# Attention plus causal convolution on one core: the out projection from exact f32 matmuls to three f32r products

## The reference, cut to what matters

```python
# x (16, 512, 1024); mask = cond (16, 1024)
q = xt @ Wq.T                                    # per batch 1024 x 512, 8 heads of 64
scores = scale * q_h @ q_h.T                     # keys = queries = values
logits = (scores * cmask + (1.0 - cmask) * -1e30) * rmask
ctx = softmax(logits) @ q_h
x = x + (ctx @ Wo.T) transposed                  # the out projection and the residual
x = x + causal_depthwise_conv(x, cond) + bias
```

## Time and profile before

| | us |
|---|---|
| median of 3 runs | 4175.13 (4171.65 to 4175.92) |
| profiled execution, its own time | 4174.45 |
| its span, first to last instruction | 4172.7 |
| TensorE busy in the span | 4055.7 (97%) |
| ScalarE busy | 2709.2 (65%) |
| GpSimd busy | 2543.2 (61%) |
| VectorE busy | 2417.5 (58%) |
| share of 16 DMA engines, main queue | 42.5% |

### The profile page before, as it was taken

How to read it: one execution, slowest core, us unless ns; L and a number is a source line. 1 busy time by engine, 2 the same in 40 slices (tenths; PEclk the granted TensorE clock), 3 DMA queues, 4 the chain that set the end, 5 groups by cost and what they waited for, 6 DMA issues and landing times. The chain is left out here.

```text
span 4172.7 us, 57357 instructions
## 1 busy us (share of the span) xinstructions
PE 4055.7 (97%) x18688; PEld 2506.5 (60%) x18688; DVE 2417.5 (58%) x2260; ACT 2709.2 (65%) x3782; POOL 2543.2 (61%) x1042
## 2 busy tenths in 40 slices
PE   7999999999999999999999999999999999999799
PEld 4665656566565655655565665556556555655598
DVE  4664555556565655656565565656556465656676
ACT  4775757667575766757576675757667575766465
POOL 4775767667575766757576675757667575766200
PEclk8999999999999999999999999999999999999999
DMA  4433434343343434344343434434433443443588
GB/s 111 106 87 91 104 94 114 91 105 92 91 105 88 117 92 101 92 94 104 86 117 92 101 92 93 108 83 117 97 97 92 97 106 81 116 97 76 147 292 265
DMA packets 308543, 451.95 MB, mean 108 GB/s; under 512 B 155043, under 2 KB 223267, under 8 KB 308134
## 3 DMA queue, kind: packets, MB, share of 16 engines
q1 hardware_dynamic: 308262, 448.18, 42.5%
HBM read 112.28 MB, written 67.11 MB: 43 GB/s over the span
## 5 line engine op out<-in xcount | busy, mean ns | idle before, releaser
L725 POOL TENSOR_TENSOR plo<-p,phi 128x1024 fp32r<-128x1024 f32 x1024 | 2539.3, 2491 | 1349.0 <-ACT phi L656 1344.1
L654 ACT ACTIVATE p<-sc 128x512 f32<-128x512 f32 x2048 | 1108.9, 594 | 815.9 <-PE sc L527 676.1
L769 DVE TENSOR_REDUCE mrow<-misc 128x1 f32<-128x1024 f32 x1024 | 1203.0, 1216 | 731.2 <-PE misc L488 731.1
L656 ACT ACTIVATE phi<-p 128x1024 fp32r<-128x1024 f32 x1024 | 1086.1, 1061 | 32.5
L526 PE MATMUL sc<-quer,keys 128*128 128x512 f32 x2048 | 912.1, 445 | 22.9 <-issue 13.1
L539 PE MATMUL pv<-phi,val 128*96 128x512 f32 x2048 | 857.5, 419 | 18.3 <-issue 18.3
L527 PE MATMUL sc<-quer,keys 96*128 96x512 f32 x2048 | 810.8, 396 | 0.0
L541 PE MATMUL pv<-phi,val 128*64 128x512 f32 x2048 | 806.4, 394 | 0.0
L545 PE MATMUL pv<-plo,val 128*96 128x512 f32 x2048 | 639.0, 393 | 0.9 <-POOL plo L725 0.9
L539 PEld LDWEIGHTS pv<-phi,val 128*96 128x96 f32 x2048 | 330.1, 161 | 339.7 <-issue 184.6
L526 PEld LDWEIGHTS sc<-quer,keys 128*128 128x128 f32 x2048 | 387.7, 189 | 192.5 <-issue 69.0
(11 more groups left out here) (70 smaller groups left out, 2823.7 us busy)
## 6 DMA issues: line engine op xcount, KB each, us to landing
keys<-hi SPq DMA_DIRECT2D x256, 256.0 KB, 3.2
quer<-mhi SPq DMA_DIRECT2D x256, 256.0 KB, 5.0
keys<-lo SPq DMA_DIRECT2D x128, 256.0 KB, 5.7
quer<-mlo SPq DMA_DIRECT2D x128, 256.0 KB, 3.8
xo<-x SPq DMA_DIRECT2D x64, 512.0 KB, 4.8
x<-xo SPq DMA_DIRECT2D x64, 512.0 KB, 4.9
xin<-x SPq DMA_DIRECT2D x16, 2048.0 KB, 13.4
out<-stage SPq DMA_DIRECT2D x64, 512.0 KB, 6.4
```

The costliest lines, as they stand in the source:

```text
L654: act.activation(p32[:, t % NP32, half(h)], sc[:, h, :], ACT.Exp, scale=SCALE).then_inc(s_p32, 1)
L656: act.activation(phi[:, t % NPHI, :], p32[:, t % NP32, :], ACT.Copy).then_inc(s_phi, 1)
L725: pool.tensor_tensor(plo[:, t % NPLO, :], p32[:, t % NP32, :], phi[:, t % NPHI, :].bitcast(F32), ALU.subtract).then_inc(s_plo, 1)
L769: reduced = dve.tensor_reduce(mrow[:, q:q + 1], misc[:, k, :], AX.X, ALU.max)
```

## The change

- `wo` (f32) goes. At the start the weight is loaded into the memory of `xo`, ScalarE writes its high part `woh` (one copy of 128 x 2048 to F32R), VectorE its low part `wol`.
- `ct` goes. The normalisation writes in place into `ca`. After the exponentials of step (p, 1, 7), ScalarE copies `ca` of the pair before to `cth[:, p]` (F32R, 128 x 1024), and after its `plo` of that step GpSimd makes `ctl[:, p]` = `ca` - `cth`.
- An out item is 12 f32r matmuls instead of 4 f32 ones: woh x cth, wol x cth, woh x ctl, 4 blocks each.
- The out items stand at other steps, and the stores of `xo` at other places of SyncE's queue.
- In the tail, high and low parts of the last pair are made by ScalarE and VectorE by halves, after both halves have been normalised.
- Memory is laid out anew (`val`, `mneg`, `mask8r` placed over the convolution's tiles, `spare` added, a smaller scratch for dynamic DMA).

```diff
-OUT_AT = {(0, 1, 7): 0, (1, 0, 0): 1, (1, 0, 2): 2, (1, 0, 4): 3,
-          (1, 0, 6): 4, (1, 1, 0): 5, (1, 1, 2): 6, (1, 1, 4): 7}
+HIGH_AT = (1, 7)
+LOW_AT = (1, 7)
+OUT_AT = {(1, 0, 2): 0, (1, 0, 3): 1, (1, 0, 5): 2, (1, 0, 7): 3,
+          (1, 1, 0): 4, (1, 1, 2): 5, (1, 1, 3): 6, (1, 1, 5): 7}
...
-                sp.dma_start(wo[:], woT.rearrange("(k p) e -> p k e", p=P)).then_inc(s_const, 16)
+                sp.dma_start(wo32, woT.rearrange("(k p) e -> p k e", p=P)).then_inc(s_woh, 16)
...
-                        if phase != "first" and (p, i) == (1, 0):
-                            store_xo(b - 1, 0)
                         if phase != "first" and (p, i) == (1, 1):
+                            store_xo(b - 1, 1)
                             load_xo(b - 1, 3, True)
...
                         if phase != "first" and (p, i) == (1, 0):
+                            store_xo(b - 1, 0)
                             load_xo(b - 1, 2, True)
-                            store_xo(b - 1, 1)
...
-                if phase == "end" and item[1] == 0:
-                    pe.wait_ge(s_half, 1)
-                elif item[1] == (1 if phase == "end" else 0):
-                    pe.wait_ge(s_cnorm, PAIRS * (prev_b + 1))
-                for k in range(PAIRS):
-                    last = pe.matmul(out, wo[:, k, m * P:(m + 1) * P], ct[:, k, half(h)],
-                                     start=(k == 0), stop=(k == PAIRS - 1))
+                if phase == "end":
+                    if item[1] < 2:
+                        pe.wait_ge(s_last_ctl, item[1] + 1)
+                elif item[1] == 0:
+                    pe.wait_ge(s_ctl, PAIRS * (prev_b + 1))
+                cols = slice(m * P, (m + 1) * P)
+                for n, (w, c) in enumerate(((woh, cth), (wol, cth), (woh, ctl))):
+                    for k in range(PAIRS):
+                        last = pe.matmul(out, w[:, k, cols], c[:, k, half(h)],
+                                         start=(n == 0 and k == 0), stop=(n == 2 and k == PAIRS - 1))
...
-                    act.wait_ge(s_cnorm, pair(b, p) - 1)
+                    act.wait_ge(s_ctl, pair(b, p) - 1)
...
+            def context_high(b, p):
+                act.wait_ge(s_cnorm, pair(b, p) + 1)
+                if not (isinstance(b, int) and b == 0):
+                    act.wait_ge(s_xo, b * 2 * DT)
+                act.activation(cth[:, p, :], ca[:, p % 2, :], ACT.Copy).then_inc(s_cth, 1)
...
+                act.wait_ge(s_woh, 16)
+                act.activation(woh[:], wo32, ACT.Copy).then_inc(s_wo_high, 1)
...
                             exponentials(b, p, i, t, first)
+                            if (i, t) == HIGH_AT and not (phase == "first" and p == 0):
+                                context_high(*before(b, p))
...
+            def context_low(b, p):
+                pool.wait_ge(s_cth, pair(b, p) + 1)
+                pool.tensor_tensor(ctl[:, p, :], ca[:, p % 2, :], cth[:, p, :].bitcast(F32), ALU.subtract).then_inc(s_ctl, 1)
...
                             split(b, p, i, t, phase == "first" and p == 0 and i == 0)
+                            if (i, t) == LOW_AT and not (phase == "first" and p == 0):
+                                context_low(*before(b, p))
...
-                dve.tensor_tensor(ct[:, p, :], ca[:, p % 2, :], den[:, p % 2, :], ALU.mult).then_inc(s_cnorm, 1)
+                dve.tensor_tensor(ca[:, p % 2, :], ca[:, p % 2, :], den[:, p % 2, :], ALU.mult).then_inc(s_cnorm, 1)
...
+            def weights_low():
+                dve.wait_ge(s_wo_high, 1)
+                dve.tensor_tensor(wol[:], wo32, woh[:].bitcast(F32), ALU.subtract).then_inc(s_wol, 1)
...
-                    dve.tensor_tensor(ct[:, p, half(h)], ca[:, p % 2, half(h)], den[:, p % 2, half(h)], ALU.mult).then_inc(done, 1)
+                    c = ca[:, p % 2, half(h)]
+                    dve.tensor_tensor(c, c, den[:, p % 2, half(h)], ALU.mult).then_inc(s_last_norm, 1)
+                for h in range(2):
+                    dve.wait_ge(s_last_cth, h + 1)
+                    if h == 0:
+                        dve.wait_ge(s_ctl, PAIRS * B - 1)
+                    dve.tensor_tensor(ctl[:, p, half(h)], ca[:, p % 2, half(h)], cth[:, p, half(h)].bitcast(F32),
+                                      ALU.subtract).then_inc(s_last_ctl, 1)
```

More of the change, by code:

```diff
@@ L131, in __init__ @@
             self.quer = sb("quer", [P, 4, T], F32R, place)
+            self.mneg = sb("mneg", [KT, P], F32R, place)
+            self.mask8r = sb("mask8r", [KT, P], F32R, place)
         self.xin = sb("xin0", [P, SLOTS, TH], F32)
@@ L140, in __init__ @@
             self.p32 = sb("p32", [P, NP32, T], F32, place)
+            self.val = sb("val", [P, 2, KT, 2, VC], F32R, place)
         with ExitStack() as place:
@@ L146, in __init__ @@
         self.brow = sb("brow", [P, T], BF16)
+        self.spare = sb("spare", [P, 2560], F32)
         self.own = sb("own", [P, CH], F32)
@@ L199, in build_attention @@
         wq = sb("wq", [P, DT, D], F32)
-        wo = sb("wo", [P, PAIRS, D], F32)
+        woh = sb("woh", [P, PAIRS, D], F32R)
+        wol = sb("wol", [P, PAIRS, D], F32R)
         ident_r = sb("ident_r", [P, P], F32R)
@@ L214, in build_attention @@
         keys, quer, keys2, quer2 = pre.keys, pre.quer, pre.keys2, pre.quer2
-        val = sb("val", [P, 2, KT, 2, VC], F32R)
+        val = pre.val
         mrow = sb("mrow", [P, KT], F32)
-        mneg = sb("mneg", [KT, P], F32R)
-        mask8r = sb("mask8r", [KT, P], F32R)
+        mneg, mask8r = pre.mneg, pre.mask8r
         p32, phi, plo = pre.p32, pre.phi, pre.plo
@@ L222, in build_attention @@
         den = sb("den", [P, 2, T], F32)
-        ct = sb("ct", [P, PAIRS, T], F32)
+        cth = sb("cth", [P, PAIRS, T], F32R)
+        ctl = sb("ctl", [P, PAIRS, T], F32R)
         xo = sb("xo", [P, 2, T], F32)
+        wo32 = xo[:].rearrange("p a t -> p (a t)").rearrange("p (k e) -> p k e", e=D)
         sc = ps("sc", [P, 2, HALF])
@@ L231, in build_attention @@
         s_begin = sem("s_begin")
-        s_half = sem("s_half")
         s_ident = sem("s_ident")
@@ L259, in build_attention @@
         s_cnorm = sem("s_cnorm")
+        s_woh = sem("s_woh")
+        s_wo_high = sem("s_wo_high")
+        s_wol = sem("s_wol")
+        s_cth = sem("s_cth")
+        s_ctl = sem("s_ctl")
+        s_last_norm = sem("s_last_norm")
+        s_last_cth = sem("s_last_cth")
+        s_last_ctl = sem("s_last_ctl")
         s_ones = sem("s_ones")
@@ L566, in start @@
                 do("start", 0, 0, "head", PHASES["start"]["head"], (0, 0, 0))
-                pe.wait_ge(s_const, 32)
+                pe.wait_ge(s_const, 16)
             def batch(phase, b):
@@ L573, in batch @@
                             first = phase == "first" and p == 0 and i == 0
+                            if phase == "first" and (p, i, t) == (1, 0, 0):
+                                pe.wait_ge(s_wol, 1)
                             scores(b, p, i, t, first)
@@ L681, in end @@
                     last_context(h)
+                p = PAIRS - 1
+                for h in range(2):
+                    act.wait_ge(s_last_norm, h + 1)
+                    act.activation(cth[:, p, half(h)], ca[:, p % 2, half(h)], ACT.Copy).then_inc(s_last_cth, 1)
             run(act, start, batch, end)
@@ L838, in start @@
                 do("start", 0, 0, "head", PHASES["start"]["head"], (0, 0, 0))
+                weights_low()
             def batch(phase, b):
@@ L891, in end @@
                 p = PAIRS - 1
-                for h, done in enumerate((s_half, s_cnorm)):
+                for h in range(2):
                     dve.wait_ge(s_cab, NH * B + h)
@@ L1082 @@
     from concourse.bass_utils import run_bass_kernel_spmd
-    nc = bacc.Bacc("TRN2", target_bir_lowering=False, num_devices=1)
+    nc = bacc.Bacc("TRN2", target_bir_lowering=False, num_devices=1, dynamic_dma_scratch_size=1024)
     arrays = {
```

## The result

Median 4107.99 us (4105.77 to 4113.86, 4 runs) against 4174.38 (4 runs) before: ratio 0.9844, interval 0.9827 to 0.9861. Forecast was 4111. The profiled execution took 4113.86, its span is 4112.1, 60.6 less than before.

| stretch | before | after | change | forecast |
|---|---|---|---|---|
| start to the first exponential | 43.51 | 43.77 | +0.26 | 0 |
| steps, to ScalarE's first copy of the last context | 3850.04 | 3785.17 | -64.9 | -65.5 |
| tail, to the convolution's first memset | 45.19 | 49.55 | +4.4 | +1.8 |
| convolution | 233.96 | 233.61 | -0.35 | 0 |

What follows compares the result with a forecast made beforehand. TensorE was taken to bound the steps, the chain of VectorE and transfers the tail. From 4174.45 us: -75.6 items, +9.6 waits, +0.5 parts, +1.8 tail gave 4110.8, said as 4111; own range 4102 to 4122, widened to 4094 to 4130.

Steps and rivals of the forecast that it cites:

- Items: Out items on TensorE: 2.80 us each instead of 3.43, 75.6 us saved over the 120 in steps.
- Rival D: Out items: f32r products of this shape run at an f32 record's distance, about 4385 us; chance 0.01.
- Waits around moved items: TensorE's waits in pair 1 and after: 2.0 us against 1.36, 0.64 given back a batch, 9.6 in 15.
- W: Time for pairs 1 and 2 together, mneg of step (0, 1, 5) to that of (2, 1, 5); 134.31 us before.
- rival A: Steps: waits do not grow, or the next step absorbs them; 4081 to 4102 us, chance 0.13.
- Parts in step (p, 1, 7): High and low parts on ScalarE and GpSimd: covered, cost 0; 0.5 us charged for the last batch's pair 3.
- Start: Making the weight's parts before the first exponential and maxima: cost 0, at worst 2 us.
- Tail: Between attention and convolution: low parts on VectorE delay its chain; cost 1.8 us, between 0 and 4.7.
- Total: Whole kernel: -63.7 us against the profiled 4174.45, so 4110.8; said as 4111.

Runs made afterwards that it cites:

- f32 items: Changed kernel with each out item as four f32 matmuls of the high parts alone, high and low parts still made; 4177.9 us, ratio 1.0006.
- places alone: Kernel before with only the out items' steps and the order of SyncE's queue changed, items left as four f32 matmuls; 4175.5 us, ratio 1.0001.
- mhi and lo first: Changed kernel with VectorE making mhi and lo before the residual in step (1, 0, 2); 4092.1 us, ratio 0.98.
- either remedy: Changed kernel with mhi and lo before the residual in (1, 0, 2), 4092.1 us, or with out items 0 to 2 at (1, 0, 4) to (1, 0, 6), 4098.3 us.
- all three: Changed kernel with mhi, lo before the residual, tail low parts on GpSimd, items 0-3 in even steps from (1, 0, 0), 30 useless tail matmuls; 4097.4 us.
- two products: Changed kernel without the product wol x cth, so 8 f32r matmuls an item instead of 12; 4067.6 us, ratio 0.9739.
- mhi and lo first, tail on GpSimd: Changed kernel with mhi and lo before the residual in (1, 0, 2) and the tail's two low parts made by GpSimd; 4086.4 us, ratio 0.9792.

## Why the prediction was right

- **Items.** 12 x 0.233 = 2.80 was met to the last digit, and f32 items and places alone confirm that nothing else carries the gain. Rival D (5.15) is out, and so are the 2.57 that the prediction worked out from the four passes in the Trainium skill, *FP8 and Floating Point Precision*, section TensorE Precision Notes.
- **Waits around moved items.** 1.52 for item 1: step (1, 0, 3) takes 7.48, and 5.94 once the wait is removed (mhi and lo first), so 1.5; it is gone with either remedy. Step (1, 0, 1) is 0.36 longer than before, for 0.37, and (1, 1, 0) takes 6.02 against 5.93 in all three, for 0.1. W was forecast as 76.7 + 53.2 = 129.9 and is 129.83. One bound of this part is added up wrongly: no waits at all would be 2.0 x 15 = 30 us better than the forecast and not 20, which is the distance from unchanged waits (rival A has it right).
- **Parts in step (p, 1, 7).** 0 forecast; W differs by 0.03 between f32 items and places alone. For the last pair, which has no projection, 0.5 was charged; from the `mneg` of (2, 1, 5) to that of (3, 0, 5) it is 23.29 against 23.12.
- **Start.** 0 forecast; +0.26, which says nothing: over all runs the first exponential starts between 42.3 and 44.5, at 42.80 in places alone.
- **Tail.** The mis-sized term: 1.8 forecast, 4.4 measured. The step that failed is "at 2.80 each the first residual is due as the tap table ends". The item took 5.26 at the lower clock, behind 10.74 us of an idle TensorE, and VectorE waited 2.73 for it. The lower clock was there before as well: the item began behind 6.12 of idle, and from 3899.6 to 3903.0 the granted clock was 0.50. But then the residual started at 3905.62, right behind the tap table, with no idle time shown, so VectorE's work hid the slow item. The stretch had shown the clock at 0.84 there, and I did not use it. The size varies: in the changed kernel run again the clock came back during the item, which took 4.18, and the tail 48.36.
- **Total.** 4110.8 forecast from the profiled execution of before; the one of after took 4113.86, 3.1 more, of which 2.6 are the tail. The median lies 6 below it, by scatter between executions: on the stretch over a change of batch (from the `mneg` of (3, 1, 5) to that of the next (0, 1, 5)) the mean over 14 batches was 55.30 in the profile after and 54.91 in the same kernel run again.
- **Luck.** That the steps came out at -64.9 for -65.5 is in part luck. W summed over 15 batches fell by 67.6, more than the forecast's 66.0; some 3.5 of this was given back, since the clock fell at four changes of batch in the profile after and at two in that of before (last section).

## What to carry to other kernels

Where an instruction of VectorE with two SBUF inputs may meet one of GpSimd, work out both starts relative to what anchors each: making the work ahead of one shorter can move it into the other's time, and then lose most of what was saved. A chain that a bank's turn leads through (reduction, bank, matmul) turns such a hold into idle time of TensorE, and a turned order on VectorE was enough to avoid it here. Work that is hidden behind another engine's wait should be looked up for every place where it runs: the one pair without a projection gave up 7.6 us where its fellows gave 0.14. Add the items' price from distances between starts, and give an item that begins behind a long idle time of TensorE (4.3 and 10.7 us here) the price at its lower clock.

## What the runs showed that I had not expected

- Saving work can cost the clock: in two products TensorE ran its item at 0.55 behind 4.3 us of idle time, in the tail at 0.50 behind 10.7; with 40 matmuls of no use in the gap the item took 2.87 us.
- The same lies behind part of the scatter of some 8 us between executions. The 14 profiles have 210 changes of batch inside the steps. In 35 of them the granted clock fell to 0.50 once, and these stretches took 56.4 to 56.9 us; in the other 175 it did not fall, and none took over 55.5. One fall costs some 1.8 us. The profile after has four and the same kernel run again one, which is 5.4 of the 7.3 us between these two executions; the fastest full version (mhi and lo first, tail on GpSimd) has none. Executions without a profile do not show it. In the batch of the profile after whose stretch took 56.41 us, TensorE was idle for 1.25 at the new batch's first step, and in the window behind it the granted clock was 0.72:
```profile
1692.00:1698.00 6.00, 6.00 (x15) 3.18 (x13) 2.07 (x2) 2.14 (x3) 4.99 (x3) 0.72 0.01 1
```
In a batch with 54.73 it stayed at 1.00 there, behind an idle time of 1.19. Why it falls in one and not in the other is not shown.
